# One more level of an addition tree on VectorE, and two transposed terms a block on TensorE in place of three

## The chip, the cores and the metric

The kernel runs on one core of one Trainium2 chip. The metric is the time of one execution on the device in microseconds (us). TensorE multiplies and transposes, VectorE (DVE) and GpSimd (POOL) add and multiply element by element, ScalarE (ACT) copies and applies functions, and SyncE (SP) issues most transfers.

## The reference, cut to what matters

The layer is a gated cross attention written as a long convolution, and after it a mixture of eight experts. Only the first half is touched:

```
kv[h,i,j,:]  = layernorm(x)[h,i,:] * ctx[h,j,:]            # 8 x 8 products a head, 16 heads of a batch row group
y            = causal convolution of kv with k[h] (length 512)  + kv * skip
out[h,j,:]   = sum over i of y[h,i,j,:] * ctx[h,i,:]
x            = x + tanh(g_xattn) * out
```

The sum over the eight values of i is what the change is about. After it each row of x goes through layernorm, a router picks one of eight experts, and the row passes through the expert's gate, up and down matrices.

## The kernel before, in words

The first block walks over G = 16 groups of 128 rows (8 batches by 16 channels, that is two heads of 8 channels for each batch). A stage g does the convolution of group g and, one stage late, the closing steps of group g-1. Time lies on the partitions in four blocks (lb) of 128 positions, and the 512 columns of a block hold 8 batches by 64 products (i, j).

In stage g each engine runs a list of instructions of its own, written out by hand, and semaphores join them:

- TensorE (`stage` at the block's tensor function): the convolution of head 0 in blocks 0, 1, 2 (`conv`, L740), the router's logits of group g-2, the turn of the skip terms, block 3 of head 0, then `sum_heads` of group g-1 (L770), then head 1 in blocks 0 to 3, then the transposes of the next x (`v_in`) and of the normed rows (`x2_in`), both L720. Every convolution matmul is 128x128 by 128x512 in three parts (high by high, low by high, high by low).
- VectorE: `product` (L634) multiplies each block of y from PSUM by the context and writes it into `prod`, whose index i runs over eight terms of 512 columns; a ninth term (index J = 8) holds the skip part. `outer` (L619) makes kv of the next group, one head at a time, 2048 columns. `add_fours` (L664) adds terms 2 and 3 to terms 0 and 1 (1024 columns). `residual` (L642) adds the sum into x.
- GpSimd: `add_pairs` (L445, 2048 columns) adds terms 4 to 7 to terms 0 to 3 of the group before; `skip_last` (L436, 512 columns) makes the ninth term; `skip_first` (L419, 256 columns, written to `vc`) and `kv_low` (L428, 2048 columns, kv less its rounded part) follow once for each head of the next group.
- ScalarE: `kv_high` (L508) rounds kv, and the norms and small copies are its too.

So the eight terms are reduced in three places: 8 to 4 on GpSimd (`add_pairs`), 4 to 2 on VectorE (`add_fours`), and the last two with the skip term on TensorE, where `sum_heads` transposes three terms for each of four blocks into one PSUM bank, adding them up as it goes: 12 matmuls of 128x128 with the identity.

The waits around the sum: `add_fours` waits for `s_add` (add_pairs). It ends with `s_add2`. `sum_heads` waits for `s_add2` and `s_skp`. `residual` waits for `s_att`, which `sum_heads` sets. `kv_low` of the next group's head 0 waits for `s_khi`, which `kv_high` sets after `outer`. The loop over groups runs two stages in a pass (u is 0 or 1), with stages 0, 1, 14 and 15 written out.

The second block (routing, then 18 or 19 tiles of sorted rows through their experts) is not touched.

Of the kernel before, what the change touches and what calls it, by code (L numbers as in the profile page):

```python
# [5 lines left out]
def flamingo_layer_kernel(  # L6
# [33 lines left out]
    ALU = mybir.AluOpType  # L40
    ACT = mybir.ActivationFunctionType
    AX = mybir.AxisListType.X

    P = 128
    G, _, L = x_rows.shape
    H = k.shape[0]
    J = 8
# [23 lines left out]
    def put(name, shape, dt=f32, at=None):  # L71
        size = 4
        for n in shape[1:]:
            size *= n
        size = (size + 31) // 32 * 32
        if at is None:
            at = place
        t = nc.alloc_sbuf_tensor_at(name, shape, dt, offset=at[0])
        at[0] += size
        return t  # L80
# [65 lines left out]
    prod = put("prod", [P, 2, J + 1, LB * P], f32, att)  # L146
# [46 lines left out]
    with ctx:  # L193
        def sem(name):
            return ctx.enter_context(nc.semaphore(name))
# [46 lines left out]
        s_add2 = sem("s_add2")  # L242
# [14 lines left out]
        def wait(eng, s, value):  # L257

            if isinstance(value, int) and value <= 0:
                return  # L260
            eng.wait_ge(s, value)
# [18 lines left out]
        def known(g, test):  # L280

            return test(g) if isinstance(g, int) else True
# [33 lines left out]
        with nc.Block() as block:  # L316
# [261 lines left out]
            def _(dve):  # L578
# [59 lines left out]
                def residual(g, u, n):  # L638

                    dve.wait_ge(s_att, g + 1)  # L640
                    dve.wait_ge(s_r[u], 16 * (n + 1))
                    nc.vector.scalar_tensor_tensor(out=x_res[:, u, :], in0=att_bank, scalar=tanh_x[:, 0:1],  # L642
                                                   in1=x_res[:, u, :], op0=ALU.mult, op1=ALU.add)\
                        .then_inc(s_x2, 1)
# [16 lines left out]
                def add_fours(g, u):  # L661

                    dve.wait_ge(s_add, G + 1 if isinstance(g, int) and g == G - 1 else g + 1)
                    nc.vector.tensor_tensor(prod[:, u, 0:2, :], prod[:, u, 0:2, :], prod[:, u, 2:4, :], ALU.add)\  # L664
                        .then_inc(s_add2, 1)

                def skip_sum(g, u):
                    dve.wait_ge(s_skip, 2 * (g + 1))
                    wait(dve, s_skf, g - 1)
                    nc.vector.tensor_reduce(skip_r[:, u, :, :],  # L670
                                            vc[:, u, :].rearrange("p (a h i) -> p a h i", h=2, i=J), AX, ALU.add)\
                        .then_inc(s_skw, 1)

                def stage(g, u, n):
                    more = known(g, lambda g: g < G - 1)
                    before = known(g, lambda g: g >= 1)
                    product(g, u, n, 0, 0)
                    product(g, u, n, 0, 1)
                    skip_sum(g, u)
                    if more:  # L680
                        outer(g + 1, 1 - u, n + u, 0)
                    product(g, u, n, 0, 2)
                    if before:
                        add_fours(g - 1, 1 - u)
                    if more:
                        outer(g + 1, 1 - u, n + u, 1)
                    product(g, u, n, 0, 3)
                    if known(g, lambda g: g < G - 2):
                        ln1(g + 2, u, n + 1)
                    if before:  # L690
                        residual(g - 1, 1 - u, n - 1 + u)
                    product(g, u, n, 1, 0)
                    if before:
                        ln2_first(g - 1, 1 - u)
                        ln2_last(g - 1)
                    product(g, u, n, 1, 1)
                    product(g, u, n, 1, 2)
                    product(g, u, n, 1, 3)
# [10 lines left out]
                stages(dve, stage)  # L709
                add_last_pairs(G - 1, 1)  # L710
                add_fours(G - 1, 1)
                residual(G - 1, 1, G // 2 - 1)
                ln2_first(G - 1, 1)
                ln2_last(G - 1)

            @block.tensor
            def _(pe):
                def transposes(bank, src, done):
                    for b in range(LB):
                        last = nc.tensor.transpose(bank[:, b * P:(b + 1) * P], src(slice(b * P, (b + 1) * P)),  # L720
                                                   ident[:, :])
                    last.then_inc(done, 1)

                def v_in(g):
                    pe.wait_ge(s_xn, g + 1)
                    wait(pe, s_kv, 2 * g)
                    transposes(v_bank, lambda cols: xn[:, cols], s_vtr)

                def conv(g, u, n, hh, blocks):
                    h = 2 * g + hh  # L730
                    for lb in blocks:
                        if lb == 0:
                            pe.wait_ge(s_klo, h + 1)
                            if hh == 0:
                                pe.wait_ge(s_t[u], 16 * (n + 1))
                        wait(pe, s_p, (h - 1) * LB + lb + 1)
                        for mb in range(lb + 1):
                            d = lb - mb
                            for n, (t, v) in enumerate(((0, kv_hi), (0, kv_lo), (1, kv_hi))):
                                last = nc.tensor.matmul(  # L740
                                    y_bank[lb][:, :], strip[:, u, 2 * hh + t, d * P:(d + 1) * P],
                                    v[:, u, hh, mb * COL:(mb + 1) * COL],
                                    start=(mb == 0 and n == 0), stop=(mb == lb and n == 2))
                        last.then_inc(s_y, 1)

                def logits_of(g):
                    pe.wait_ge(s_xn2T, g + 1)
                    wait(pe, s_logc, g)
                    pe.wait_ge(s_skc, min(g + 2, G) if isinstance(g, int) else g + 2)
                    for b in range(LB):  # L750
                        last = nc.tensor.matmul(log_bank, xn2T[:, b, :], router[:, b, :],
                                                start=(b == 0), stop=(b == LB - 1))
                    last.then_inc(s_log, 1)

                def skip_turn(g, u):

                    pe.wait_ge(s_skw, g + 1)
                    wait(pe, s_skc, g)
                    nc.tensor.matmul(skip_bank, flip[:, :], skip_r[:, u, :, :].rearrange("p a h -> p (a h)"),
                                     start=True, stop=True).then_inc(s_skf, 1)  # L760

                def sum_heads(g, u):

                    pe.wait_ge(s_add2, g + 1)
                    pe.wait_ge(s_skp, g + 1)
                    wait(pe, s_x2, g)
                    terms = [0, 1, J]
                    for lb in range(LB):
                        for i in terms:
                            last = nc.tensor.matmul(att_bank[:, lb * P:(lb + 1) * P],  # L770
                                                    prod[:, u, i, lb * P:(lb + 1) * P], ident[:, :],
                                                    start=(i == 0), stop=(i == J), is_transpose=True)
                    last.then_inc(s_att, 1)

                def x2_in(g, u):
                    pe.wait_ge(s_xn2, g + 1)
                    wait(pe, s_xn2T, g)
                    transposes(x2T_bank, lambda cols: xn2[:, u, cols], s_x2tr)

                def stage(g, u, n):  # L780
                    before = known(g, lambda g: g >= 1)
                    conv(g, u, n, 0, (0, 1, 2))
                    if known(g, lambda g: g >= 2):
                        logits_of(g - 2)
                    skip_turn(g, u)
                    conv(g, u, n, 0, (3,))
                    if before:
                        sum_heads(g - 1, 1 - u)
                    conv(g, u, n, 1, range(LB))
                    if known(g, lambda g: g < G - 2):  # L790
                        v_in(g + 2)
                    if before:
                        x2_in(g - 1, 1 - u)

                pe.wait_ge(s_const, 7)
                v_in(0)
                v_in(1)
                stages(pe, stage)
                logits_of(G - 2)
                sum_heads(G - 1, 1)  # L800
                x2_in(G - 1, 1)
                logits_of(G - 1)
# [487 lines left out]
```

## Time and profile before

| | |
|---|---|
| median of 3 runs | 732.05 us (730.9 to 732.33) |
| the profiled execution, its own time | 732.09 us |
| its span in the profile | 730.3 us |
| granted TensorE clock over the span | 0.962 |
| busy TensorE | 657.3 us (90%) |
| busy weight loads | 537.7 us (74%) |
| busy VectorE | 512.6 us (70%) |
| busy GpSimd | 556.2 us (76%) |
| busy ScalarE | 242.1 us (33%) |

An engine's busy time is the sum over its instructions' spans. Line numbers (L664) are lines of the kernel before. In a timeline row the first two numbers are the start and the duration in us, then come the engine and the line, and in square brackets at the end the idle time ahead of the instruction and what ended it. A GpSimd span is rough; the starts of GpSimd instructions that follow one another without a wait are firmer. A matmul's span holds its way through the array, so matmuls overlap: their pace is read from the starts.

### The profile page before, as it was taken

What the parts mean: (1) busy time and instruction counts of PE and PEld (TensorE: products, weight loads), DVE (VectorE), ACT (ScalarE), POOL (GpSimd) and SP (SyncE); (2) the same over time, 40 slices, a digit from 0 to 9 for tenths busy, and PEclk for the clock granted to TensorE, in tenths of its full rate; (3) what the DMA queues carried; (4) which work ended last, traced back from release to release, by engine and by line L of the source; (5) the groups of instructions that cost most, each with busy time, mean ns of one, the idle gap of its engine ahead of it and who ended that gap; (6) DMA issues with size and microseconds to landing.
All of it is one profiled execution on the core that took longest, in us unless ns stands there. A gap on an engine that the chain in (4) does not pass through costs nothing.

```text
span 730.3 us, 11087 instructions
## 1 busy us (share of the span) xinstructions
PE 657.3 (90%) x3168; PEld 537.7 (74%) x3169; DVE 512.6 (70%) x661; ACT 242.1 (33%) x350; POOL 556.2 (76%) x359
## 2 busy tenths in 40 slices
PE   0989999999999999768388989999999999999973
PEld 0868888888888888567266868887888888888853
DVE  5688888888888887566099968598979938532300
ACT  3533443333333442132123323333333333333330
POOL 1799999999999999117177768798888878775852
PEclk9999999999999999869779999999999999999996
DMA  7135566666666553039776665466766655441110
GB/s 225 55 115 159 159 160 165 165 160 177 174 176 161 158 149 111 29 123 255 133 246 213 242 196 172 159 196 200 237 211 206 197 165 179 145 131 28 57 43 5
DMA packets 50239, 113.86 MB, mean 156 GB/s; under 512 B 5900, under 2 KB 6092, under 8 KB 50224
## 3 DMA queue, kind: packets, MB, share of 16 engines
q1 hardware_dynamic: 41920, 95.68, 42.9%
q0 software_dynamic: 4320, 12.60, 6.5%
q10 hardware_dynamic: 3984, 5.40, 2.6%
q8 instruction: 7, 0.11, 0.1%
q14 instruction: 8, 0.07, 0.0%
HBM read 94.33 MB, written 20.90 MB: 158 GB/s over the span
## 4 chain that ended last, share of the span: by engine, by line
PE 39%; DVE 8%; issue 4%; POOL 4%; DMA 2%; ACT 0%; DVEq 0%; POOLq 0%; ACTq 0%
PE pair L1203 23%; PE bank L1216 13%; POOL sorted_x L943 2%; PE bank L1236 2%; DVE up L1029 2%; DMA sorted_x<-xn_all,pos 2%; DVE down_hi L1029 1%; DVE gate L1029 1%; PE bank L1192 1%; DVE down_lo L1032 1%; DVE up L1032 1%; DVE gate L1032 1%; DMA raw<-down_w 1%; DVE select L882 0%; POOL ys L1137 0%
## 5 line engine op out<-in xcount | busy, mean ns | idle before, releaser
L740 PE MATMUL bank<-kv_hi,strip 128*128 128x512 f32 x640 | 214.8, 405 | 0.0
L428 POOL TENSOR_TENSOR kv_lo<-kv,kv_hi 128x2048 fp32r<-128x2048 f32 x31 | 143.8, 4640 | 14.3 <-ACT kv_hi L508 14.3
L740 PEld LDWEIGHTS bank<-kv_hi,strip 128*128 128x128 f32 x640 | 122.0, 191 | 29.1
L740 PE MATMUL bank<-kv_lo,strip 128*128 128x512 f32 x320 | 128.3, 401 | 0.0
L634 DVE TENSOR_TENSOR prod<-bank,cT 128x512 f32<-128x512 f32 x128 | 85.1, 683 | 32.3 <-PE bank L740 28.7
L1203 PE MATMUL pair<-gate,xT_hi 128*128 x304 | 99.6, 409 | 5.8 <-DVE xT_lo L1038 3.6
L508 ACT ACTIVATE kv_hi<-kv 128x2048 fp32r<-128x2048 f32 x32 | 61.4, 1920 | 121.6 <-DVE kv L619 92.2
L1203 PE MATMUL pair<-up,xT_hi 128*128 x304 | 95.7, 396 | 3.2 <-DVE up L1032 3.2
L1029 DVE CAST down_hi<-raw 128x1024 fp32r<-128x1024 f32 x32 | 33.9, 1059 | 72.3 <-PE bank L1216 49.4
L619 DVE TENSOR_TENSOR kv<-pair,cK 128x2048 f32<-128x2048 f32 x32 | 72.9, 2279 | 0.4 <-PE pair L720 0.4
L1154 POOL TENSOR_TENSOR hid<-hid,mid 128x1024 f32<-128x1024 f32 x19 | 49.5, 2605 | 29.7 <-ACT mid L1083 29.6
L1203 PEld LDWEIGHTS pair<-gate,xT_hi 128*128 128x128 f32 x304 | 57.5, 194 | 19.4 <-issue 6.7
L1216 PE MATMUL bank<-down_hi,hT_hi 128*128 128x512 f32 x152 | 62.6, 412 | 8.7 <-POOL hT_lo L1164 5.7
L740 PEld LDWEIGHTS bank<-kv_lo,strip 128*128 128x128 f32 x320 | 61.1, 191 | 12.0
L1203 PEld LDWEIGHTS pair<-up,xT_hi 128*128 128x128 f32 x304 | 57.1, 188 | 17.3 <-issue 3.6
L445 POOL TENSOR_TENSOR prod<-prod 128x2048 f32<-128x2048 f32 x15 | 69.2, 4610 | 0.2 <-DVE prod L634 0.2
L1203 PE MATMUL pair<-gate,xT_lo 128*128 x152 | 61.3, 403 | 0.0
L1216 PE MATMUL bank<-down_hi,hT_lo 128*128 128x512 f32 x152 | 60.6, 399 | 0.0
L1216 PE MATMUL bank<-down_lo,hT_hi 128*128 128x512 f32 x152 | 60.5, 398 | 0.0
L1203 PE MATMUL pair<-up,xT_lo 128*128 x152 | 60.2, 396 | 0.0
L1032 DVE TENSOR_TENSOR down_lo<-raw,down_hi 128x1024 fp32r<-128x1024 f32 x32 | 54.7, 1708 | 1.1
L1032 DVE TENSOR_TENSOR up<-raw,up 128x1024 fp32r<-128x1024 f32 x28 | 54.1, 1930 | 1.0
(153 smaller groups left out, 1096.1 us busy)
## 6 DMA issues: line engine op xcount, KB each, us to landing
strip<-kparts SPq DMA_DIRECT2D x16, 1024.0 KB, 6.0
raw<-gate_w SPq DMA_DIRECT2D x32, 512.0 KB, 3.8
raw<-up_w SPq DMA_DIRECT2D x32, 512.0 KB, 4.5
raw<-down_w SPq DMA_DIRECT2D x32, 512.0 KB, 4.3
sorted_x<-fill SPq DMA_DIRECT2D x14, 513.0 KB, 5.8
xs<-sorted_x ACTq DMA_DIRECT2D x20, 256.5 KB, 2.9
x_in<-x_back SPq DMA_DIRECT2D x16, 256.0 KB, 5.4
cK<-ctx_back SPq DMA_DIRECT2D x16, 256.0 KB, 5.2
```

Source lines behind the costliest of these rows:

```text
L428: nc.gpsimd.tensor_tensor(kv_lo[:, u, hh, :], kv[:, hh, :], kv_hi[:, u, hh, :].bitcast(f32), ALU.subtract).then_inc(s_klo, 1)
L445: nc.gpsimd.tensor_tensor(prod[:, u, 0:J // 2, :], prod[:, u, 0:J // 2, :], prod[:, u, J // 2:J, :], ALU.add).then_inc(s_add, 1)
L508: nc.scalar.activation(kv_hi[:, u, hh, :], kv[:, hh, :], ACT.Copy).then_inc(s_khi, 1)
L619: nc.vector.tensor_tensor(kv[:, hh, :].rearrange("p (a i j) -> p a i j", i=J, j=J), v.unsqueeze(3).broadcast_to([P, LB * NB, J, J]), c.uns ...
L634: nc.vector.tensor_tensor(dst[:, :, :, hh * J:(hh + 1) * J], y_bank[lb][:, :].rearrange("p (b i j) -> p b i j", i=J, j=J), c, ALU.mult).th ...
L740: last = nc.tensor.matmul(y_bank[lb][:, :], strip[:, u, 2 * hh + t, d * P:(d + 1) * P], v[:, u, hh, mb * COL:(mb + 1) * COL], start=(mb == ...
L943: nc.gpsimd.indirect_dma_start(out=sorted_x[:, :], out_offset=bass.IndirectOffsetOnAxis(ap=pos[:, g:g + 1], axis=0), in_=xn_all[:, g, :], ...
L1029: nc.vector.tensor_copy(hi, raw[:, c, :]).then_inc(s_whi, 1)
L1032: nc.vector.tensor_tensor(lo, raw[:, c, :], hi.bitcast(f32), ALU.subtract)\
L1154: nc.gpsimd.tensor_tensor(hid[:, :], hid[:, :], mid[:, :], ALU.mult).then_inc(s_hid, 1)
L1203: last = nc.tensor.matmul(bank[:, half * 512:(half + 1) * 512], a[:, b, :], weights[:, bass.ds(o, 512)], start=(b == 0 and n == 0), stop=( ...
L1216: last = nc.tensor.matmul(out_bank[:, :], a[:, b, :], w[:, b * 512:(b + 1) * 512], start=(b == 0 and n == 0), stop=(b == IB - 1 and n == 2))
```

## The change

A function `add_twos` is added on VectorE. It waits until `add_fours` of the same group has set `s_add2`, adds term 1 to term 0 (512 columns, both from SBUF), and sets `s_add2` again. It stands right behind `add_fours`, ahead of the second `outer`. TensorE waits for the second count, and transposes terms 0 and J alone: 8 matmuls in place of 12.

```
+                def add_twos(g, u):
+
+                    dve.wait_ge(s_add2, 2 * g + 1)
+                    nc.vector.tensor_tensor(prod[:, u, 0, :], prod[:, u, 0, :], prod[:, u, 1, :], ALU.add)\
+                        .then_inc(s_add2, 1)
...
                     if before:
                         add_fours(g - 1, 1 - u)
+                    if before:
+                        add_twos(g - 1, 1 - u)
                     if more:
                         outer(g + 1, 1 - u, n + u, 1)
...
                 add_fours(G - 1, 1)
+                add_twos(G - 1, 1)
                 residual(G - 1, 1, G // 2 - 1)
...
-                    pe.wait_ge(s_add2, g + 1)
+                    pe.wait_ge(s_add2, 2 * (g + 1))
                     pe.wait_ge(s_skp, g + 1)
                     wait(pe, s_x2, g)
-                    terms = [0, 1, J]
+                    terms = [0, J]
```

VectorE in the middle of a stage of the loop, before (L619 is `outer`, L634 `product`, L664 `add_fours`, in the first loop stage):

```order
L619 TENSOR_TENSOR kv<-pair,cK 128x2048 [waits s_skip,s_klo,s_khi]
L630 REGISTER_ALU
L634 TENSOR_TENSOR prod<-bank,cT 128x8x8x8 [waits s_y]
L664 TENSOR_TENSOR prod<-prod 128x1024 [waits s_add]
L619 TENSOR_TENSOR kv<-pair,cK 128x2048 [waits s_skip,s_klo,s_khi]
```

The same place now (L670 is `add_twos`):

```order
L619 TENSOR_TENSOR kv<-pair,cK 128x2048 [waits s_skip,s_klo,s_khi]
L630 REGISTER_ALU
L634 TENSOR_TENSOR prod<-bank,cT 128x8x8x8 [waits s_y]
L664 TENSOR_TENSOR prod<-prod 128x1024 [waits s_add]
L670 TENSOR_TENSOR prod<-prod 128x512 [waits s_add2]
L619 TENSOR_TENSOR kv<-pair,cK 128x2048 [waits s_skip,s_klo,s_khi]
```

One instruction with a wait on the one ahead of it has come in; the second `outer` and all that follows it stand behind it.

TensorE around the sum, before (L740 is the convolution, L770 the sum):

```order
L740 MATMUL bank<-kv_lo,strip 128x512
L740 MATMUL bank<-kv_hi,strip 128x512
L770 MATMUL pair<-ident,prod 128x128 [waits s_skp,s_add2]
L770 MATMUL pair<-ident,prod 128x128 x11
L740 MATMUL bank<-kv_hi,strip 128x512 [waits s_p,s_klo]
```

And now (the same lines are L749 and L779):

```order
L749 MATMUL bank<-kv_lo,strip 128x512
L749 MATMUL bank<-kv_hi,strip 128x512
L779 MATMUL pair<-ident,prod 128x128 [waits s_skp,s_add2]
L779 MATMUL pair<-ident,prod 128x128 x7
L749 MATMUL bank<-kv_hi,strip 128x512 [waits s_p,s_klo]
```

Four transposes have gone; the place of the sum in TensorE's queue and its waits are as they were.

## Rows read from the trace of the kernel before

**Rows 1.** Windows: busy time by engine, granted clock, DMA share, GB/s.

```profile
45.40:291.00 245.60, 245.23 (x1253) 202.12 (x1254) 208.63 (x344) 97.67 (x137) 232.99 (x85) 0.99 0.56 155
46.80:50.30 3.50, 3.50 (x12) 2.73 (x11) 2.88 (x8) 2.08 (x3) 3.50 (x1) 0.52 0.00 0
```

**Rows 2.** Timeline: first instructions of three sums (stages 1, 6, 14) on TensorE.

```profile
45.56 1.53 PE L770 MATMUL pair<-ident,prod 128*128 128x128 f32 x12 [2.54 <-DVE prod L664]
...
134.61 1.49 PE L770 MATMUL pair<-ident,prod 128*128 128x128 f32 x12
...
291.72 1.48 PE L770 MATMUL pair<-ident,prod 128*128 128x128 f32 x12
```

**Rows 3.** Timeline of stage 7, all engines, the instructions around the sum.

```profile
139.93 4.61 POOL L428 TENSOR_TENSOR kv_lo<-kv,kv_hi 128x2048 fp32r<-128x2048 f32 x1
...
142.33 0.82 ACT L482 ACTIVATE xn<-x_res,nb,rs 128x512 f32<-128x512 f32 x1 [0.48 <-DVE nb L595]
...
142.96 1.04 PE L720 MATMUL pair<-ident,xn 128*128 128x128 f32 x8
...
144.51 4.59 POOL L445 TENSOR_TENSOR prod<-prod 128x2048 f32<-128x2048 f32 x1
...
146.15 0.69 DVE L634 TENSOR_TENSOR prod<-bank,cT 128x512 f32<-128x512 f32 x1 [0.72 <-PE bank L740]
...
147.35 2.28 DVE L619 TENSOR_TENSOR kv<-pair,cK 128x2048 f32<-128x2048 f32 x1
...
149.06 1.08 POOL L436 TENSOR_TENSOR prod<-cT,skip_w 128x512 f32<-128x512 f32 x1
...
150.10 0.91 POOL L419 TENSOR_TENSOR vc<-kv,skip_b 128x256 f32<-128x256 f32 x1
...
150.15 1.95 DVE L664 TENSOR_TENSOR prod<-prod 128x1024 f32<-128x1024 f32 x1
...
151.84 4.70 POOL L428 TENSOR_TENSOR kv_lo<-kv,kv_hi 128x2048 fp32r<-128x2048 f32 x1 [0.84 <-ACT kv_hi L508]
...
152.14 1.29 PEld L770 LDWEIGHTS pair<-ident,prod 128*128 128x128 f32 x12 [0.45 <-DVE prod L664]
...
157.39 4.61 POOL L428 TENSOR_TENSOR kv_lo<-kv,kv_hi 128x2048 fp32r<-128x2048 f32 x1
```

**Rows 4.** The line of the fours: durations min/median/max in ns, first and last start.

```profile
L664 DVE TENSOR_TENSOR prod<-prod x16: 1224/1864/2092, 43.4 to 302.3; 128x1024 f32<-128x1024 f32 x16
```

**Rows 5.** Timelines of VectorE and GpSimd in the expert block: three meetings.

```profile
475.62 3.81 DVE L1032 TENSOR_TENSOR down_lo<-raw,down_hi 128x1024 fp32r<-128x1024 f32 x1
475.94 2.40 POOL L1164 TENSOR_TENSOR hT_lo<-mid,hT_hi 128x1024 fp32r<-128x1024 f32 x1
...
507.33 2.34 DVE L1032 TENSOR_TENSOR down_lo<-raw,down_hi 128x1024 fp32r<-128x1024 f32 x1
507.30 1.29 POOL L1137 TENSOR_TENSOR ys<-ys,x2s 128x512 f32<-128x512 f32 x1
...
391.38 1.23 DVE L1032 TENSOR_TENSOR up<-raw,up 128x1024 fp32r<-128x1024 f32 x1
391.42 2.34 POOL L1137 TENSOR_TENSOR ys<-ys,x2s 128x512 f32<-128x512 f32 x1
```

**Rows 6.** Timelines of GpSimd and VectorE in stage 1.

```profile
43.33 1.09 POOL L436 TENSOR_TENSOR prod<-cT,skip_w 128x512 f32<-128x512 f32 x1
44.36 1.84 POOL L419 TENSOR_TENSOR vc<-kv,skip_b 128x256 f32<-128x256 f32 x1
...
43.42 2.08 DVE L664 TENSOR_TENSOR prod<-prod 128x1024 f32<-128x1024 f32 x1 [1.41 <-POOL prod L445]
```

**Rows 7.** Timelines of VectorE and GpSimd in stage 2.

```profile
62.34 0.91 POOL L419 TENSOR_TENSOR vc<-kv,skip_b 128x256 f32<-128x256 f32 x1 [0.23 <-DVE kv L619]
62.66 1.67 DVE L664 TENSOR_TENSOR prod<-prod 128x1024 f32<-128x1024 f32 x1
64.37 4.61 POOL L428 TENSOR_TENSOR kv_lo<-kv,kv_hi 128x2048 fp32r<-128x2048 f32 x1 [1.12 <-ACT kv_hi L508]
```

## The prediction, made before the changed kernel ran

> **What bounds the kernel now.** First I read the windows: in the convolution stages with a sum, 45.4 to 291 us, TensorE is busy 245.23 of 245.60 us at a granted clock of 0.99, GpSimd 232.99 us [rows 1]. Neither has room to give. Then the starts of the sums: 45.56 in stage 1, 291.72 in stage 14 + 1 = 15 [rows 2], so 14 stages take (291.72 - 45.56) / 14 = 17.58 us each.
>
> Last the timeline of one stage, 7 [rows 3]. VectorE waits for a block of y at 146.15, then runs without a break: the product, `outer` for head 0 (to 147.35 + 2.28 = 149.63), another product, and the fours, 150.15 to 152.10. The sum starts at 152.14. TensorE's weight loads waited 0.45 us for the fours, though its own pipeline hides most of that. So the two engines arrive nearly together, and whatever is added to VectorE ahead of the sum falls on TensorE.
>
> The second thing to see is the fours' own time: 1224 ns at least, 1864 in the median [rows 4]. At 150.15 GpSimd had been at `vc` since 150.10; it ended at 151.01, and the fours ended at 152.10, 1.09 later [rows 3]. The same in the expert block: an addition of the same size took 3.81 us, to 479.43, where a GpSimd operation of 2.40 us ran until 478.34: again 1.09 later [rows 5]. So a VectorE addition with both inputs in SBUF and a GpSimd operation exclude each other for the whole of an instruction. `outer`, the products and the residual, with one input in PSUM, are not held up. In the convolution the fours are the one frequent VectorE instruction that meets this.
>
> The Trainium skill says the same of the port that the two share (SBUF — State Buffer, Who interferes with whom): an exclusive lock, whoever issues first has it for the whole instruction. The trace agrees with 3.81 us. What it doesn't state is who gets it where one has been waiting, which decides below.
>
> **The change part by part.**
>
> Taken off: four of 12 transposes. Twelve weight loads took 1.29 us [rows 3], so 0.43 us a stage. All of it does not come through. `x2_in` waits for the norm that ends at 142.33 + 0.82 = 143.15, 8.54 us after its sum at 134.61 [rows 2, 3]; the block of L720 starts at 142.96 and its second half, `x2_in`, 0.4 later, at 143.36. With 0.43 less ahead of it TensorE would stand there at 142.93, 0.2 to 0.3 us early. Net 0.2 us on the way from the sum to the next products. The convolution behind it starts earlier by that.
>
> Added: 512 columns. The fours' streaming and overhead are 1.224 us unhindered for 1024 [rows 4], of which 1.09 follow once the port is free. At one column a cycle, the half is 0.55 us once the port is free and about 0.69 in all with nothing in the way, plus 0.03 for the wait on the fours. (Bounds: 0.5 and 1.2, half and whole of the fours.) That alone would be 0.72 - 0.2 to 0.4, some +0.3 to +0.6 a stage.
>
> The wait for the port is the large term. Behind the fours GpSimd's next work is `kv_lo` of head 0, 4.6 us in one instruction. It starts at 151.84, when `kv_hi` is done, 2.21 us behind the end of `outer` at 149.63 [rows 3]; the twos start at 152.10 + 0.03 = 152.13. `kv_lo` is first by 0.3 us. Then the twos wait until 152.10 + (151.84 + 4.70 - 152.10) = 156.54 and end at 157.1, and the sum starts 5.0 us late. Queued behind the twos on VectorE are `outer` for head 1, the last product of head 0, both norms, the residual and head 1's products; behind the sum on TensorE all of head 1's convolution. That is the loss in one stage; the stages after it shift, and who is first must be asked again there. I go by T, the start of a sum, and T', the next.
>
> Who wins a meeting: at 507.30 GpSimd against 507.33 VectorE, VectorE took 2.34 (it waited); at 391.38 VectorE against 391.42 GpSimd, GpSimd took 2.34 [rows 5]. So the earlier start wins, by as little as 0.03. Where both are queued, the one that waited gets it: in stage 1 the fours waited for `skip_last` (43.33 to 44.42) and went ahead of `vc`, which started at 44.36 and took 1.84 [rows 6].
>
> *Stage 1.* The fours end at 45.50 and `vc` holds the port to 44.36 + 1.84 = 46.20. The twos end at 46.75 instead of the fours at 45.50: +1.25, sure whatever follows. No `kv_lo` is ahead of them.
>
> *A stage after a long TensorE idle* (5 us). In the trace an idle of 2.54 us ahead of the sum at 45.56 [rows 2] was followed by 3.5 us at a granted clock of 0.52, the 1.2 GHz level [rows 1]. The same 1.2 GHz stretch costs about 3.5 x 0.48 = 1.7 us on TensorE. Stage 2 shows the result: from 45.56 to the fours at 62.66 are 17.1 us [rows 2, 7], where the ordinary is 150.15 - 134.61 = 15.54 [rows 2, 3]. Then `outer` ends at 62.66 - 0.52 = 62.14, GpSimd is free and waiting, `vc` runs 62.34 to 63.25, the fours end at 64.33, the twos would start at 64.36, and `kv_lo` starts at 64.37 [rows 7]. A tie, with VectorE ahead by 0.01. If the twos win: T' is T + 16.9 (fours) + 1.67 + 0.03 + 0.69 + 0.05 = T + 19.4. If they lose: T + 16.9 + 1.7 + 4.6 + 0.6 = T + 23.9.
>
> *A stage after a short idle.* GpSimd's `kv_lo` was held by the twos until T. Its queue then takes: from 152.10 to the second `kv_lo` at 157.39, 5.29; 4.58 and 4.55 for that and the pairs (139.93, 144.51, 149.06), 1.04 for `skip_last` [rows 3]; `vc` at T + 15.4. The fours start at T + 15.54 - 0.2 = T + 15.3, plus 0.1 in every second stage, at the loop's turn: T + 15.3 to 15.5. Again a tie. If the fours are first, they wait for `skip_last` (T + 15.45), end at 16.5, `vc` follows to 17.2, and the twos, waiting, take the port ahead of `kv_lo` and end at 17.8: T' = T + 17.8. If `vc` is first, the fours end at T + 17.4 while `kv_lo` has been waiting since 14.9 + 2.2 = 17.1; it runs 4.5 and the twos end at T + 22.4, with a TensorE idle of some 5 us, hence the slow clock next.
>
> *Sum.* I take it that the first tie goes to VectorE in 6 of 10 and the second to GpSimd in 7 of 10. Then a stage after a long idle takes 0.6 x 19.4 + 0.4 x 23.9 = 21.2 on average, one after a short idle 0.3 x 17.8 + 0.7 x 22.4 = 21.0, so 21.1 for each of 13 stages: 13 x (21.1 - 17.58) = +46. Stage 1 +1.3. In the last but one interval there is no `kv_lo` any more, only `skip_last` between fours and twos: +1 to +2. At the very end the twos cost 0.72, and four transposes less give back 0.43 to 0.8: 0. Sum +49 on the profiled execution's 732.09, which stands at the median (732.05): 781.
>
> The Trainium skill warns (Perfetto Trace Analysis, GPSIMD Engine Instruction) that a GpSimd span in a profile is unreliable and start-to-start spacing is to be used. The rows differ little there: 4.61 by span and 4.58 by spacing for the same `kv_lo`; over 13 stages that is 0.4 us.
>
> **Rivals.**
> 1. *Every addition loses.* Both ties go to `kv_lo`: each stage 23.9. 13 x (23.9 - 17.58) = 82, + 3: 817. For it: in stage 7 the lead of `kv_lo` is 0.3 us. Against: after the slow clock the twos are level.
> 2. *Short waits only.* The order fours, `vc`, twos, `kv_lo` holds once reached: 17.8 a stage, 13 x 0.22 = 3, + 2.5: 737. Or the 512 columns meet no exclusion and cost their 0.6 each: 15 x 0.6 = 9: 741. For it: stage 1 starts in that order. Against: `vc` and the fours are level.
> 3. *Not slower.* VectorE keeps the port from the fours over to the twos, 0.03 us apart, though `vc` is queued. Then with the fours ending at T + 16.5 the twos end at 17.3, and TensorE, which by itself needs 17.58 - 0.43 + 0.2 = 17.35 a stage, sets the time: 13 x -0.23 = -3, so 729. It decides if the port isn't passed to a waiting GpSimd in 0.03 us; against it stands `vc`'s 1.84, which shows the passing at an end of `skip_last`, and that it was had back at once when the fours ended.
> 4. *The transposes' 0.43 us come through whole and the twos are covered*: 15 x -0.43 = -6, 726. Against: fours and sum stand 0.04 apart (152.10, 152.14), with nothing to cover 0.7.
>
> **Chances.** Mixed outcome, 745 to 808: 0.58, which gives the time. Rival 1, above 808: 0.14. Rival 2, 733.5 to 745: 0.22. Rivals 3 and 4: 0.04, and 0.02 for no change. About 0.2% (1.5 us) is what a measurement of this kernel tells from none. Faster 0.03, same 0.02, slower 0.95. The range, 739 to 818, leaves out rivals 3 and 4, the low end of 2 and the top of 1, some 0.15. The mixed outcome's own range is 760 to 800.
>
> **What would show it.** In the profile after: L670, 16 instructions, with a median far above 0.7 us, and single ones of 4.5 to 5.3 us that end 0.55 us after a `kv_lo`; TensorE idle ahead of L779 of 40 us or more, against almost nothing; a granted clock well under 0.99 in the convolution; the expert block as long as before. Stage 1's sum at 46.8. If L670 takes 0.7 in all, there is no exclusion and the time is near 741; if all are 1 to 1.4 us with `vc` in between, rival 2; if all are 5, rival 1. The forecast is wrong if VectorE's wait is broken up, GpSimd taking turns with it within an instruction.

## The result, and the profile after

The changed kernel takes 791.62 us (median of 4 runs, 782.64 to 793.88), the kernel before, run beside it, 731.47 (4 runs, 730.07 to 732.33). The ratio is 1.080, 95% interval 1.072 to 1.089. The four runs lie 11 us apart, where the four of before lie 2.3 apart; that alone says little, since in three of the four sets run beside the experiments (9 to 17 executions) the kernel before scatters by 7 to 10 us itself. The profiled execution took 793.88 us, its span is 792.1, 61.8 more than before (730.3).

All of it is in the convolution. The last sum starts at 365.49 where it started at 303.59, 61.9 later; from there to the end are 426.6 us against 426.7. (The lines of `add_fours` and above keep their numbers; the twos are L670, the convolution is L749, the sum L779.)

The line of the twos, then that of the fours (duration min/median/max in ns, then first and last start in us):

```profile
L670 DVE TENSOR_TENSOR prod<-prod x16: 691/4929/5036, 45.4 to 364.7; 128x512 f32<-128x512 f32 x16
```

```profile
L664 DVE TENSOR_TENSOR prod<-prod x16: 1224/1678/2087, 43.2 to 363.5; 128x1024 f32<-128x1024 f32 x16
```

The fours are as they were [rows 4]. The twos take 0.69 us at best, and 4.9 in the median.

Two lines of the table of waits (who waited for whom, us in total, times, longest):

```profile
PE pair L779 <- DVE prod L670: 51.3, 16, 4.9
POOL vc L419 <- DVE kv L619: 44.4, 21, 8.5
```

TensorE stands 51 us ahead of its sums, where it stood 3.7 in the kernel before. GpSimd, whose `kv_lo` held the port, waits too: `outer` is queued behind the twos, and `vc` waits for `outer`.

Two windows: from the start of sum 1 to that of the last transposes of sum 16, and the 5 us behind one long idle. The columns are TensorE, its weight loads, VectorE, ScalarE and GpSimd (busy us, with the number of instructions), then the granted clock, the DMA share and GB/s. [Rows 1] had a clock of 0.99 for the stages, and 0.52 behind stage 1's idle alone.

```profile
46.61:366.80 320.19, 271.20 (x1256) 220.96 (x1257) 265.52 (x372) 100.08 (x142) 237.54 (x85) 0.91 0.44 119
70.07:75.00 4.93, 4.93 (x16) 4.27 (x17) 4.33 (x9) 2.10 (x3) 1.45 (x2) 0.52 0.01 3
```

Now the meetings themselves, from the timelines of VectorE, GpSimd and TensorE (start and duration in us first), to be held against [rows 3]. Stage 6, which follows a short idle:

```profile
146.91 0.91 POOL L419 TENSOR_TENSOR vc<-kv,skip_b 128x256 f32<-128x256 f32 x1
147.22 1.69 DVE L664 TENSOR_TENSOR prod<-prod 128x1024 f32<-128x1024 f32 x1
148.92 4.50 POOL L428 TENSOR_TENSOR kv_lo<-kv,kv_hi 128x2048 fp32r<-128x2048 f32 x1 [1.10 <-ACT kv_hi L508]
148.94 5.02 DVE L670 TENSOR_TENSOR prod<-prod 128x512 f32<-128x512 f32 x1
...
154.02 1.97 PE L779 MATMUL pair<-ident,prod 128*128 128x128 f32 x8 [4.82 <-DVE prod L670]
```

`kv_lo` starts 0.02 us ahead of the twos and has the port until 153.42. The twos end at 153.96, 0.54 later, and the sum starts 0.06 behind them.

Stage 5, which follows a long idle:

```profile
128.75 0.91 POOL L419 TENSOR_TENSOR vc<-kv,skip_b 128x256 f32<-128x256 f32 x1 [0.23 <-DVE kv L619]
129.07 1.66 DVE L664 TENSOR_TENSOR prod<-prod 128x1024 f32<-128x1024 f32 x1
130.77 0.69 DVE L670 TENSOR_TENSOR prod<-prod 128x512 f32<-128x512 f32 x1
130.77 5.15 POOL L428 TENSOR_TENSOR kv_lo<-kv,kv_hi 128x2048 fp32r<-128x2048 f32 x1 [1.12 <-ACT kv_hi L508]
```

Here both start at 130.77 by the record. The twos take 0.69, and `kv_lo` takes 5.15 where it needs 4.5 to 4.6: it waited. The two meetings differ by 0.02 us in who starts first, and by 4.3 us in the length of the twos.

The 14 intervals from sum 1 to sum 15 (T' - T, from the start of one sum to the next), in order: 23.46, 19.74, 22.56, 19.14, 22.51, 24.72, 24.33, 24.15, 24.02, 19.61, 22.54, 19.08, 22.35, 18.47. By kind, against the forecast:

| interval | forecast T' - T | measured | how often |
|---|---|---|---|
| after a long idle, twos win | 19.4 | 19.1 to 19.7 | 4 |
| after a long idle, twos lose | 23.9 | 24.0 to 24.7 | 4 |
| after a short idle, twos lose | 22.4 | 22.4 to 22.6 | 4 |
| after a short idle, twos win | 17.8 | none | 0 |
| stage 2 (lost) | as after a long idle | 23.46 | 1 |
| last, no `kv_lo` | +1 to +2 | 18.47 (16.96 before) | 1 |

### The profile page after: what moved, and what is told of

Same layout as the page of the kernel before. It is cut to its first block, busy times and chain, and to the rows that moved or that the text cites. A ratio compares the mean times of both kernels' runs of the same rounds, so it can differ in the third digit from the quotient of the medians.

```text
span 792.1 us, 10981 instructions
## 1 busy us (share of the span) xinstructions
PE 671.3 (85%) x3104; PEld 546.4 (69%) x3105; DVE 561.7 (71%) x677; ACT 242.2 (31%) x350; POOL 560.6 (71%) x359
## 4 chain that ended last, share of the span: by engine, by line
PE 36%; DVE 7%; issue 4%; POOL 3%; DMA 2%; ACT 0%; DVEq 0%; POOLq 0%; ACTq 0%
PE pair L1212 21%; PE bank L1225 12%; POOL sorted_x L952 2%; PE bank L1245 2%; DVE up L1038 1%; DMA sorted_x<-xn_all,pos 1%; DVE down_hi L1038 1%; DVE gate L1038 1%; PE bank L1201 1%; DVE down_lo L1041 1%; DVE up L1041 1%; DVE gate L1041 1%; DMA raw<-down_w 1%; DVE select L891 0%; POOL ys L1146 0%
## 5 line engine op out<-in xcount | busy, mean ns | idle before, releaser
L749 PE MATMUL bank<-kv_hi,strip 128*128 128x512 f32 x640 | 223.6, 420 | 0.2
L749 PEld LDWEIGHTS bank<-kv_hi,strip 128*128 128x128 f32 x640 | 128.3, 200 | 31.3 <-issue 0.9
L749 PE MATMUL bank<-kv_lo,strip 128*128 128x512 f32 x320 | 132.4, 414 | 0.0
L634 DVE TENSOR_TENSOR prod<-bank,cT 128x512 f32<-128x512 f32 x128 | 86.0, 684 | 44.8 <-PE bank L749 41.2
L749 PEld LDWEIGHTS bank<-kv_lo,strip 128*128 128x128 f32 x320 | 64.6, 202 | 12.8
L619 DVE TENSOR_TENSOR kv<-pair,cK 128x2048 f32<-128x2048 f32 x32 | 73.0, 2281 | 0.4 <-PE pair L729 0.4
L1212 PEld LDWEIGHTS pair<-gate,xT_hi 128*128 128x128 f32 x304 | 57.5, 194 | 19.3 <-issue 6.5
L779 PE MATMUL pair<-ident,prod 128*128 128x128 f32 x128 | 26.3, 373 | 51.3 <-DVE prod L670 51.3
L419 POOL TENSOR_TENSOR vc<-kv,skip_b 128x256 f32<-128x256 f32 x32 | 29.8, 930 | 44.4 <-DVE kv L619 44.4
L779 PEld LDWEIGHTS pair<-ident,prod 128*128 128x128 f32 x128 | 20.8, 193 | 57.8 <-DVE prod L670 57.8
```

The costliest lines, as they stand in the source:

```text
L419: nc.gpsimd.tensor_tensor(v, same, s_g.unsqueeze(1).broadcast_to([P, LB * NB, J]), ALU.mult)\
L619: nc.vector.tensor_tensor(kv[:, hh, :].rearrange("p (a i j) -> p a i j", i=J, j=J), v.unsqueeze(3).broadcast_to([P, LB * NB, J, J]), c.uns ...
L634: nc.vector.tensor_tensor(dst[:, :, :, hh * J:(hh + 1) * J], y_bank[lb][:, :].rearrange("p (b i j) -> p b i j", i=J, j=J), c, ALU.mult).th ...
L749: last = nc.tensor.matmul(y_bank[lb][:, :], strip[:, u, 2 * hh + t, d * P:(d + 1) * P], v[:, u, hh, mb * COL:(mb + 1) * COL], start=(mb == ...
L779: last = nc.tensor.matmul(att_bank[:, lb * P:(lb + 1) * P], prod[:, u, i, lb * P:(lb + 1) * P], ident[:, :], start=(i == 0), stop=(i == J) ...
L1212: last = nc.tensor.matmul(bank[:, half * 512:(half + 1) * 512], a[:, b, :], weights[:, bass.ds(o, 512)], start=(b == 0 and n == 0), stop=( ...
```

## The experiments

**1. What the transposes are worth by themselves.**

```
-                    terms = [0, 1, J]
+                    terms = [0, J]          # no add_twos
```

> The kernel before with 8 transposes a block and no add_twos (term 1 is left out of the sum). Port theory (the whole loss comes from add_twos waiting for kv_lo at the shared port): no loss, and what the four transposes are worth shows alone: TensorE gains 0.43 us less the 0.2 to 0.3 that x2_in waits for its norm, 14 x 0.25 = 3.5, so 728.5 (726 to 731). Rival (fewer transposes shift TensorE and by that the stages' meeting at the port, fours against kv_lo, which loses time without the twos): 740 or more. If the four transposes came through whole: 725.5.

Measured: 726.7 us, ratio 0.991 (0.988 to 0.994), in the range. No loss, as the port theory has it. Of the profile's gain of 5.4 us of span, 2.3 lie in the convolution (last sum at 301.29, not 303.59) and 3.1 behind it, where other numbers are routed (that this makes the 3.1 is not shown); so the four transposes gain 2.3, and 6 had been taken away. One thing was not expected. Twice the fours took 2.8 us, 0.7 longer than the longest of before [rows 4], and TensorE then stood 0.9 us ahead of the sum; this is the second:

```profile
148.14 2.85 DVE L664 TENSOR_TENSOR prod<-prod 128x1024 f32<-128x1024 f32 x1
```

```profile
147.92 1.12 POOL L436 TENSOR_TENSOR prod<-cT,skip_w 128x512 f32<-128x512 f32 x1
148.96 0.94 POOL L419 TENSOR_TENSOR vc<-kv,skip_b 128x256 f32<-128x256 f32 x1
```

The fours waited from 148.14, `skip_last` ended at 149.04, and `vc` had the port next. What the forecast took from [rows 6], that the one that has waited goes first, isn't always so (see the last section).

**2. The twos with all transposes kept.**

```
-                    terms = [0, J]
+                    terms = [0, 1, J]       # add_twos stays
```

> The changed kernel with add_twos, but all 12 transposes kept (term 1 is counted twice). Port theory: as the changed kernel, 780 to 800, with sums 0.43 us longer; the ties come out as they will, since all of GpSimd's, ScalarE's and VectorE's work is the same. Rival (the loss comes from taking transposes away): about 742, 0.7 us x 15 over the kernel before.

Measured: 832.88 us, ratio 1.133 (1.125 to 1.142), outside both expectations. The profile tells why: with other numbers the rows are routed to 21 tiles of the expert block and not 19, and from the last sum (368.23) to the end are 466.4 us. The last sum itself starts 64.6 us later than before, in the changed kernel 61.9. So the total proves nothing; the convolution's part says that the loss is there with all the transposes in place. Four of 13 meetings of the twos with `kv_lo` were won and nine lost, as many as in the changed kernel, in another order.

**3. The same addition with one input from PSUM.**

```
-  nc.vector.tensor_tensor(prod[:, u, 0, :], prod[:, u, 0, :], prod[:, u, 1, :], ALU.add)
+  nc.vector.tensor_tensor(prod[:, u, 0, :], v_bank,           prod[:, u, 1, :], ALU.add)
```

> The changed kernel, but add_twos takes its first input from PSUM (the bank of v, which holds other numbers; term 1 is an input still), so that it reads SBUF once; size, place, waits and semaphores are the same. Port theory: no wait for kv_lo, 0.68 us each as the products of the same size take, L670 at 0.7 in all 16, time 732 + 15 x (0.71 - 0.2 to 0) = 740 to 743. Rival (the wait on the fours or the place in VectorE's queue is what costs 5 us): as the changed kernel, about 790.

Measured: 739.2 us, ratio 1.011 (1.007 to 1.014), 0.8 below the range. The line of the twos:

```profile
L670 DVE TENSOR_TENSOR prod<-pair,prod x16: 690/691/693, 44.6 to 309.1; 128x512 f32<-128x512 f32 x16
```

Sixteen times 0.69 us, with size, place and waits as in the changed kernel. And here `kv_lo` started ahead of the twos in all 13 meetings, by 0.01 to 0.30 us; the first of them:

```profile
63.70 4.59 POOL L428 TENSOR_TENSOR kv_lo<-kv,kv_hi 128x2048 fp32r<-128x2048 f32 x1 [1.10 <-ACT kv_hi L508]
```

```profile
63.72 0.69 DVE L670 TENSOR_TENSOR prod<-pair,prod 128x512 f32<-128x512 f32 x1
```

The order that costs 4.3 us in the changed kernel costs nothing. This is the run that settles it: what costs 50 us is the second input in SBUF. The last sum starts at 309.88, 6.3 us later than before; that is what a VectorE instruction of this size costs here in plain time, less what the transposes give back.

**4. `kv_lo` made to wait for the twos.**

```
 def kv_low(g, u, hh):
     ...
+    if hh == 0:
+        wait(eng, s_add2, 2 * (g - 1))
```

> The changed kernel, and GpSimd's kv_lo of head 0 waits for the twos of the group before (a semaphore wait more, nothing left out). The port is then never given to kv_lo ahead of the twos. Port theory: L670 at 0.7 us, or up to 1.6 where vc stands between, kv_lo starts some 1 us later than before, GpSimd becomes the bound at about 18.2 us a stage (17.58 before): 732 + 14 x 0.6 + 2 = 743 (738 to 748). Rival (VectorE's chain lost by anything else): about 790 as the changed kernel, since nothing else is altered.

Measured: 745.03 us, ratio 1.018 (1.012 to 1.023), in the range. One wait more, and 47 us less than the changed kernel, with the same arithmetic. The line of the twos:

```profile
L672 DVE TENSOR_TENSOR prod<-prod x16: 691/1246/1448, 45.3 to 315.1; 128x512 f32<-128x512 f32 x16
```

**5. `kv_lo` of head 0 in two halves.**

```
+ nc.gpsimd.tensor_tensor(kv_lo[..., 0:half], kv[..., 0:half], kv_hi[..., 0:half], ALU.subtract).then_inc(s_half, 1)
+ eng.wait_ge(s_half, g)
+ nc.gpsimd.tensor_tensor(kv_lo[..., half:], kv[..., half:], kv_hi[..., half:], ALU.subtract).then_inc(s_klo, 1)
```

> The changed kernel with kv_lo of head 0 made in two halves of 1024 columns, the second waiting for the first. Port theory with a wait handed over at the end of an instruction: a lost meeting costs half a kv_lo, 2.3 us, not 4.6; L670 in a lost stage at 2.7, and TensorE's idle of some 2.5 us slows the clock in fewer stages. Lost stages at about T + 20.1, so 732 + 13 x 1.5 to 2.6 + 3 = 755 to 768. Rival (a stall of fixed length, from the semaphore or the shift of the stages): about 790.

Measured: 767.76 us, ratio 1.050 (1.047 to 1.054), at the upper end of the range. The profiled execution took 772.16; in it the fours of stage 1 were kept from the port twice running, by `vc` and by the first half of `kv_lo`, and took 5.15 us (43.14 to 48.29), which put sum 1 at 51.10 and not near 46.6. The other three took 765.9 to 768.5. The twos again:

```profile
L677 DVE TENSOR_TENSOR prod<-prod x16: 691/2711/2878, 48.3 to 342.5; 128x512 f32<-128x512 f32 x16
```

A lost meeting costs 2.7 to 2.9 us in place of 5.0: the price follows the length of the one GpSimd instruction. The clock was spared in three of nine stages: TensorE's idle was 2.6 to 2.9 us in all of them, and in six a lower clock followed. Behind the idle of 2.81 us that ended at 109.55 the granted clock is 0.72 and 0.59 in the next two windows of 2.5 us, then 1.00 (behind one of the same length at 231.15 it stayed at 1.00):

```profile
109.55:112.00 2.45, 2.45 (x12) 2.12 (x13) 2.45 (x2) 0.18 (x1) 2.30 (x2) 0.72 0.65 190
112.00:114.50 2.50, 2.50 (x8) 1.98 (x7) 1.90 (x8) 1.94 (x3) 1.35 (x2) 0.59 0.00 0
```

**6. Two one-column instructions on GpSimd.**

```
 def skip_first(g, u, hh):
+    if hh == 0: nc.gpsimd.tensor_tensor(mark_pool[:, 1:2], ones[:, 0:1], ones[:, 0:1], ALU.mult)
 def kv_low(g, u, hh):          # after the wait for kv_hi
+    if hh == 0: nc.gpsimd.tensor_tensor(mark_pool[:, 0:1], ones[:, 0:1], ones[:, 0:1], ALU.mult)
```

> The changed kernel with two GpSimd instructions of one column (0.15 to 0.2 us each) per stage: one ahead of vc, one ahead of kv_lo of head 0, after its wait for kv_hi. Theory of the ties (who is first by hundredths of a us decides 4.6 us): both ties go to VectorE in every stage, L670 never above 1.7, 17.8 to 18.2 a stage, 737 to 745: work added, 50 us less. Rival (the loss is no matter of order): 790 plus 14 x 0.3 = 794.

Measured: 776.92 us, ratio 1.062 (1.060 to 1.064). Both expectations missed: below the changed kernel, but far off 737 to 745. After each long idle the twos won. After a short one they lost in 5 of 7 stages: the instruction ahead of `vc` moved `vc` by only 0.14 us, and in the five lost stages, where the loop turns, the fours came later than I had reckoned, 15.7 us after the sum. In one of these the fours had even started ahead of `vc`:

```profile
227.42 0.22 POOL L417 TENSOR_TENSOR mark_pool<-ones 128x1 f32<-128x1 f32 x1
227.57 0.94 POOL L424 TENSOR_TENSOR vc<-kv,skip_b 128x256 f32<-128x256 f32 x1
```

```profile
227.52 2.07 DVE L671 TENSOR_TENSOR prod<-prod 128x1024 f32<-128x1024 f32 x1
```

The one-column instruction held the port at 227.52, and `vc`, not the waiting fours, followed it.

**7. Only the one ahead of `kv_lo`.** (The second of the two edits above.)

> The changed kernel with only the one-column instruction ahead of kv_lo of head 0. Theory of the ties: after a long idle VectorE always wins (T + 19.4), after a short one vc still goes ahead of the fours and kv_lo is queued before they end, so it loses (T + 22.4): the two alternate, 20.9 a stage, seven long twos of 5 us; 732 + 13 x 3.3 + 3 = 778 (770 to 785), below the changed kernel's 790. Rival (losses come at random): about 790 with runs that differ by 10 us.

Measured: 773.23 us, ratio 1.058 (1.055 to 1.061), in the range. An instruction was added, and the kernel is 18 us faster than the changed one. The two kinds alternate from sum 2 on: 22.51, 19.31, 22.51, 18.90, 22.54, 20.22, 22.50, 19.43, 22.50, 18.99, 22.47, 20.19. One of the won meetings, at 107:

```profile
107.01 0.20 POOL L429 TENSOR_TENSOR mark_pool<-ones 128x1 f32<-128x1 f32 x1 [1.10 <-ACT kv_hi L510]
107.16 5.08 POOL L430 TENSOR_TENSOR kv_lo<-kv,kv_hi 128x2048 fp32r<-128x2048 f32 x1
```

```profile
107.03 0.71 DVE L672 TENSOR_TENSOR prod<-prod 128x512 f32<-128x512 f32 x1
```

The twos start 0.02 us behind the one-column instruction, wait for its 0.2 us (which costs them 0.02: 0.71 in place of 0.69) and have the port ahead of `kv_lo`, which would be due 0.13 us later: so in all six stages after a long idle. After a short one the fours and `vc` start within 0.06 us of each other, and all six were lost. In one of the six the fours were ahead of `vc` by 0.01 us (81.40 against 81.41) and `vc` still had the port. The four executions lie 4.8 us apart.

**8. Fours and twos in one instruction with one input.**

```
-  nc.vector.tensor_tensor(prod[:, u, 0:2, :], prod[:, u, 0:2, :], prod[:, u, 2:4, :], ALU.add)
+  nc.vector.tensor_reduce(prod[:, u, J // 2, :], prod[:, u, 0:4, :].rearrange("p i l -> p l i"), AX, ALU.add)
...
-                    terms = [0, 1, J]
+                    terms = [J // 2, J]
```

> The fours and the twos in one tensor_reduce over four terms (2048 elements read from one SBUF input, 512 written over term 4, which is free by then); 8 transposes. Port theory: an instruction with one SBUF input doesn't wait for GpSimd, so L664 takes a constant 2.2 us where the fours took 1.7 to 1.95, and GpSimd is never held: TensorE's sum about 0.3 to 0.45 later, less the 0.2 of fewer transposes: 732 + 14 x 0.1 to 0.25 = 733 to 736. Rival (reads of four terms 2 KB apart run slower than one element a cycle): 4 us and more each, 760.

Measured: 773.43 us, ratio 1.060 (1.056 to 1.064): the rival's case, 13 us above its figure. The line:

```profile
L664 DVE TENSOR_REDUCE prod<-prod x16: 3619/3810/3821, 43.0 to 340.0; 128x512 f32<-128x2048 f32 x16
```

2048 elements in 3.8 us are 1.86 ns each, fixed part included; the additions go at (1.224 - 0.69) / 512 = 1.04 ns an element. The wait for the port has gone: the longest is 3.82 us beside `kv_lo`'s 4.5, and the last, with GpSimd at rest, still takes 3.62. TensorE now idles 1.9 us ahead of each of sums 2 to 14, and behind 11 of these 13 idles the clock came down. What that costs shows in the interval from sum 2, behind one of the two idles that left the clock at 1.00: 19.27 us, where the eleven others took 20.5 to 20.6. One window behind an idle that brought it down:

```profile
109.00:111.50 2.50, 2.50 (x8) 1.93 (x8) 1.90 (x8) 2.00 (x2) 1.36 (x3) 0.60 0.12 44
```

**9. The same with the sum behind block 0 of head 1.**

```
+                    conv(g, u, n, 1, (0,))
                     if before:
                         sum_heads(g - 1, 1 - u)
-                    conv(g, u, n, 1, range(LB))
+                    conv(g, u, n, 1, range(1, LB))
```

> As the one with the reduce, and TensorE does block 0 of head 1's convolution (0.8 us) ahead of the sum. What stands between is then covered: TensorE never waits for the reduce, and its own work sets the stage, 17.42 - 0.43 + 0.2 = 17.2 to 17.3 against 17.58: 732 - 14 x 0.3 = 728 (726 to 731), the first that beats the kernel before. Rival (VectorE or GpSimd is the bound by then): 732 to 736, as without the move.

Measured: 757.21 us, ratio 1.037 (1.033 to 1.042). Both expectations missed, for the same reason, the reduce's 3.8 us. The move itself is worth 16 us here. By the intervals that is nearly all the clock: with the idle down to 1.24 us it stays up in all 13 stages, an interval is 19.3 to 19.6 us, as the one of run 8 with the clock up, and 11 times the 1.2 us between that one and the others are 13 to 14 us.

```profile
86.14:105.72 19.58, 17.55 (x87) 13.97 (x87) 17.12 (x26) 7.17 (x10) 16.68 (x7) 1.00 0.55 152
```

**10. The move in the kernel before.** (Only the sum's place is changed, as in 9; three terms and the fours as they were.)

> The kernel before with the sum moved behind block 0 of head 1 and nothing else: three terms, fours as they were. Expected: the 0.1 to 0.16 us of idle ahead of the sum go, 14 x 0.1 = 1.4: 730.6 (729 to 732). Whatever the reduce kernel with the same move gains beyond this comes from the transposes.

Measured: 729.34 us against 729.11 beside it, ratio 1.0003 (0.998 to 1.003): no gain that can be measured, in the range.

**11. The move in the kernel where `kv_lo` waits.** (The edits of 4 and 9.)

> The kernel in which kv_lo waits for the twos (745.0 us), and TensorE does block 0 of head 1 (0.8 us) ahead of the sum. Two theories on what sets its 18.3 us a stage. GpSimd is the bound (its own work of 16.5 us start to start, plus the fours' or twos' port time and the wait of kv_lo): TensorE's move gains nothing, 743 to 746, and the spacing of kv_lo stays at 18.3. TensorE's wait for the twos is the bound: 0.7 us less a stage, 17.6, so 735.

Measured: 743.83 us, ratio 1.013 (1.009 to 1.018); 745.03 without the move, each beside its own runs of the kernel before. GpSimd's queue sets the pace there: of the 182.8 us between sums 4 and 14 it is busy 172.1, and the rest is mostly `kv_lo` waiting for the twos. Its second `kv_lo` of three stages, from its timeline:

```profile
144.18 4.61 POOL L430 TENSOR_TENSOR kv_lo<-kv,kv_hi 128x2048 fp32r<-128x2048 f32 x1
...
162.40 4.61 POOL L430 TENSOR_TENSOR kv_lo<-kv,kv_hi 128x2048 fp32r<-128x2048 f32 x1
...
180.67 4.59 POOL L430 TENSOR_TENSOR kv_lo<-kv,kv_hi 128x2048 fp32r<-128x2048 f32 x1
```

18.2 and 18.3 us apart, while TensorE's wait has only moved, from the sum to the transposes of x:

```profile
138.66 1.09 PE L781 MATMUL pair<-ident,prod 128*128 128x128 f32 x8 [0.17 <-DVE prod L672]
147.28 0.66 PE L731 MATMUL pair<-ident,xn 128*128 128x128 f32 x4 [0.80 <-ACT xn L484]
```

So even with the order put right, no version with the true twos came nearer than 11 us to the kernel before: GpSimd needs some 16.6 us a stage for its own work (by [rows 3] three of 4.6, 1.04 and two of 0.9), and where a VectorE addition with two SBUF inputs has the port, it waits (`vc` at 154.33 in this run took 1.90 in place of 0.9).

## Why the prediction was right

**What bounds, and the lock.** Right. The two engines arrived together, and the twos fell on TensorE whole. That two SBUF inputs are the cause was argued from three rows in the prediction; run 3 shows it (0.69 us in all sixteen with one input in PSUM, though `kv_lo` was ahead in all 13 meetings), and run 5 shows that the price is the length of the GpSimd instruction.

**Stage 1, +1.25.** Measured: from the fours' start to the sum 46.61 - 43.24 = 3.37, before 45.56 - 43.42 = 2.14, so +1.23.

**The four kinds of interval.** Three were met to within 0.8 us (table above); the fourth didn't occur in the changed kernel. In run 6 it occurred twice, with intervals of 18.2 where 17.8 was forecast, one-column instructions included. The slow clock's share, put at 1.7 us a stage, shows in the two losing kinds: 24.3 on average after a long idle, 22.5 after a short one, 1.8 apart. It isn't one size, as the prediction took it to be: over the 5 us behind the long idles of sums 6 to 9 the granted clock was 0.50 to 0.54 and the intervals, all lost, took 24.72 down to 24.02; behind those of sums 4 and 12 it was 0.66 and 0.67, and the intervals, both won, took 19.14 and 19.08. Two slips change nothing: the terms of the first two kinds add up to 19.3 and 23.8, not 19.4 and 23.9, and the sum at 291.72 is the fifteenth, as the prediction counts it, where [rows 2] says 14.

**The chances of the two ties.** Here the size was off, in both, and each makes about 0.4 to 0.5 us of what an average interval is over the forecast. "The first tie goes to VectorE in 6 of 10": 4 of 9 in the profiled run, stage 2 among them. Six of ten was a guess, and 4 of 9 doesn't contradict it; who wins it is a matter of hundredths of a us that the prediction could not reckon. "The second to GpSimd in 7 of 10": 4 of 4, and 6 of 6 in run 7. For this one a step can be named, the start of the fours after a short idle, "T + 15.3, plus 0.1 in every second stage, at the loop's turn". It was 15.7 where the loop turns (105.57 - 89.81 = 15.76) and 15.4 elsewhere (run 7); `vc` stood at 15.43, as forecast:

```profile
105.24 0.94 POOL L419 TENSOR_TENSOR vc<-kv,skip_b 128x256 f32<-128x256 f32 x1
105.57 1.69 DVE L664 TENSOR_TENSOR prod<-prod 128x1024 f32<-128x1024 f32 x1
```

In the changed kernel three of the four short idles had the loop's turn behind them; the fourth, behind sum 13, is followed by a stage written out, the fours came at 15.43, 0.04 us behind `vc`, and lost too. The mean interval was 22.17 and not 21.1: 13 x 1.07 = 14 us, which takes the forecast from 781 to 795, against 793.9 for that execution. Another of its executions took 782.6, which two or three ties gone the other way would do: a won meeting in place of a lost one is 4 to 5 us by the table. That the runs differ by ties is argued; only one of them has a trace. The mechanism carried the forecast; how near to 781 the time would fall was left to these two chances, and so is partly luck.

**The rivals.** Rival 1 (every addition loses, 817) and rival 2 (short waits, 737) did not come; run 4 makes rival 2's order by a wait, and takes 745. Rivals 3 and 4 fell: the port was never kept over the 0.03 us between fours and twos where GpSimd was queued for it, and what the transposes give back by themselves is 2.3 us of 6 in the convolution (run 1).

**The gain that was meant.** Four transposes of 0.107 us, 15 times, are 6.4 us; in run 1, without the twos, 2.3 came through.

## What to carry to other kernels

Before an elementwise instruction is moved to VectorE, look at where its inputs lie and at what GpSimd does at that time: with both inputs in SBUF its price is not its own length but that of the GpSimd instruction that may stand before it (here 0.55 us of work and 4.5 of waiting). Where two engines start for the same thing within hundredths of a us, one wait on a semaphore that fixes their order was worth 47 us of the 60 lost. The scatter of a kernel's executions is no safe sign of such ties: the changed kernel's was 11 us, and that of the kernel before, over 17 executions, 10. An idle gap on TensorE that ends in a slow clock costs more than its length: 1.2 us more an interval in run 8.

## What the runs showed of the hardware that was not expected

**Who gets the port at a tie.** In the changed kernel the twos won when they started 0.00 to 0.02 us ahead of `kv_lo`, and lost when 0.01 to 0.05 behind (in stage 14, 0.48). Between the twos and `kv_lo` the earlier start decided down to the resolution of the record, in runs 2, 5 and 7 too; of the nine level ones in the changed kernel and runs 2 and 5, seven were won, and one was lost in each of the two runs. Between the fours and `vc` it did not: 0.01 us ahead (run 7) and level (once each in runs 4 and 5) the fours lost. There `vc` came right behind another GpSimd instruction, `skip_last`, in whose last 0.05 us the fours had started.

**A waiting VectorE is sometimes passed over.** In the traces of the kernels before and after and of runs 1 to 7 there are 54 cases in which a fours or twos started while a GpSimd instruction ran, waited for it, and was there before the next one, which followed at once. In 47 VectorE had the port next, 1.08 us (fours) or 0.55 us (twos) before its end; in seven GpSimd's next instruction had it. Three of the seven are those of the paragraph above. In the other four, two of them in run 1, VectorE had come 0.10 to 0.22 us behind the start of the GpSimd instruction, and no offset tells them apart: in run 1 it came 0.19 to 0.22 us behind in five stages, and was passed over in two of them. What decides it stays open.

**TensorE's clock.** Ahead of sums 2 to 14, all nine idle gaps of 4.8 to 5.0 us of the changed kernel were followed by a granted clock of 0.50 to 0.72 over the next 5 us; so were six of nine gaps of 2.6 to 2.9 us (run 5) and 11 of 13 of 1.9 us (run 8). None of 13 gaps of 1.24 us (run 9) was, nor any of 0.5 us. So between 1.9 and 2.9 us the length of the gap alone doesn't tell, and even behind the long ones the low stretch varied: 0.50 over 5 us at sum 6, 0.67 at sum 12.

**A reduce over terms 2 KB apart** takes 1.8 to 1.9 ns an element (3.62 us for 2048 with GpSimd at rest, 3.81 beside `kv_lo`). A reduce over neighbours in the kernel before, 512 elements to 64, takes 0.67 us, 1.3 ns each with the fixed part. That the distance between the terms makes the difference is argued; no run changes it alone.
